# Adjacency stored for every second block of edges, index and weight per slot for the others

## What is computed

```python
# network 0, three layers (SAGE)
msg = relu(x[src] + edge_attr_16 @ emb)
s   = segment_sum(msg, dst, N)
x   = relu(s / count @ Wl + bl + x @ Wr)
# network 1, two layers (GIN)
agg = segment_sum(edge_weight[:, None] * x[src], dst, N)
x   = relu(agg @ W1.T) @ W2.T
# network 2: x[dst] * edge_attr_64 summed by dst; network 3: three attention layers
```

## Time and profile before

| | us |
|---|---|
| three runs | 12265.70, 12251.78, 12268.37 |
| median | 12265.7 |
| the profiled execution | 12279.62 |
| its span, first to last instruction | 12277.8 |
| first pass, in the trace | about 128 to 2830 |
| sage1, sage2 | 2900 to 3567, 3605 to 4258 |
| gin0, gin1 | 4327 to 4934, 4984 to 5600 |
| attention layers | 5760 to the end |

### The profile page before, as it was taken

How to read it: one execution, slowest core, us unless ns; L and a number is a source line. 1 busy time by engine, 2 the same in 40 slices (tenths; PEclk the granted TensorE clock), 3 DMA queues, 4 the chain that set the end, 5 groups by cost and what they waited for, 6 DMA issues and landing times. The chain is left out here.

```text
span 12277.8 us, 247904 instructions
## 1 busy us (share of the span) xinstructions
PE 9079.1 (74%) x82847; PEld 7960.6 (65%) x82848; DVE 7900.3 (64%) x23163; ACT 4425.0 (36%) x9728; POOL 7910.9 (64%) x8013
## 2 busy tenths in 40 slices
PE   4888888888989888886666666666666666666665
PEld 4777777776878788884555555455555555555554
DVE  6777777777989811105666666666666666666667
ACT  2545554454444300002333333333333333333332
POOL 5666666663767564551777777477777747777773
PEclk9888888888999999896555555555555555555555
DMA  4666666665989777672333333233333323333332
GB/s 140 185 185 183 185 185 186 183 176 151 260 223 254 208 262 258 222 261 67 95 95 96 96 96 96 64 94 96 96 96 96 96 64 94 96 96 96 96 96 53
DMA packets 1267061, 1740.59 MB, mean 142 GB/s; under 512 B 234569, under 2 KB 1001892, under 8 KB 1265547
## 3 DMA queue, kind: packets, MB, share of 16 engines
q1 hardware_dynamic: 610634, 718.01, 18.9%
q10 hardware_dynamic: 400704, 723.04, 18.7%
q0 software_dynamic: 254464, 283.59, 12.5%
HBM read 1366.51 MB, written 357.22 MB: 140 GB/s over the span
## 5 line engine op out<-in xcount | busy, mean ns | idle before, releaser
L2043 POOL DMA_INDIRECT rows<-gat_table,wgt x2457 | 2339.1, 952 | 962.3 <-issue 747.9
L2043 POOL DMA_INDIRECT Y<-gat_table,wgt x2394 | 2281.1, 953 | 729.6 <-issue 729.6
L937 POOL DMA_INDIRECT bins<-scratch,slots x1288 | 1316.6, 1022 | 960.5 <-issue 672.4
L2056 PE MATMUL scores<-ident,rep 128*128 128x128 f32 x2436 | 611.0, 428 | 1093.4 <-ACT rep L2139 1093.4
L2056 PE MATMUL scores<-ident,scratch 128*128 128x128 f32 x2415 | 605.7, 428 | 1030.3 <-ACT scratch L2139 1030.3
L2097 PE MATMUL bank<-sel,msg 128*72 128x32 f32 x9702 | 1308.6, 309 | 0.0
L1280 ACT ACTIVATE xT<-xT 112x256 f32<-112x256 f32 x1716 | 711.5, 415 | 1529.6 <-DVE xT L1122 1092.7
L2097 PEld LDWEIGHTS bank<-sel,msg 128*72 128x72 f32 x9702 | 1215.6, 237 | 44.5
L2056 PEld LDWEIGHTS scores<-ident,rep 128*128 128x128 f32 x2436 | 471.8, 223 | 1149.7 <-ACT rep L2139 1149.7
L1117 DVE TENSOR_TENSOR xT<-counts,xT 112x480 f32<-112x480 f32 x1716 | 1113.7, 649 | 118.6 <-issue 92.9
L1004 PE MATMUL bank<-xT 112*64 112x120 f32 (+1 forms) x13728 | 1166.1, 280 | 27.5 <-ACT xT L1280 26.3
(11 more groups left out here) (265 smaller groups left out, 19105.6 us busy)
## 6 DMA issues: line engine op xcount, KB each, us to landing
work<-in_dst_rows SPq DMA_DIRECT2D x693, 448.0 KB
xT<-bins ACTq DMA_DIRECT2D x1716, 119.0 KB
adj<-work ACTq DMA_DIRECT2D x598, 240.0 KB
work<-adj ACTq DMA_DIRECT2D x184, 780.0 KB
xT<-adj ACTq DMA_DIRECT2D x184, 780.0 KB
work<-near_table SPq DMA_DIRECT2D x1118, 128.0 KB
near_table<-work SPq DMA_DIRECT2D x598, 128.0 KB
bins<-zeros ACTq DMA_DIRECT2D x46, 1547.0 KB
```

The source lines that it names most:

```text
L937: nc.gpsimd.indirect_dma_start(bins, bass.IndirectOffsetOnAxis(slots[u % 2][:, r * G + j:r * G + j + 1], 0), binf[r][:, j, :], None).then_ ...
L2043: nc.gpsimd.indirect_dma_start(rows[s][:, j, :], None, gat_table, bass.IndirectOffsetOnAxis(edge_sources[:, g * G + j:g * G + j + 1], 0)). ...
L2056: last = nc.tensor.transpose(score_banks[s % 2][:, j * P:(j + 1) * P], reps[s % 2][:, j, :], ident[:])
```

## The change

Blocks with even number keep their adjacency as before; the table `adj` has 23 entries. For the odd blocks no `turned_cells`, `weigh`, `adjacency` or `keep` is run. In their place ACT copies the destination and the weight of each slot (`note`, 112 x 8 numbers a piece) and stores them once a block in `notes`.

`gin_pass` then takes one even and one odd block together, 23 pairs. The even block is summed from its adjacency as before, now into two halves in turn, with five load buffers in place of eight. The odd block is summed as sage1 does: `near_table` is loaded on the SP queue, `fetch` (three bf16 parts), `far_cells` and a new `weigh` (a multiplication by the weight) on DVE, `add_cells` into two halves, with rings of three buffers. DVE adds four half sums for each pair. The bf16 parts have to be made: `sage_dense(2)` and `gin_dense0` now split `x` too. The other loops are unchanged.

```diff
-        adj = dram("adj", (NBK, P, TS * MW))
+        adj = dram("adj", (PAIRS, P, TS * MW))
+        notes = dram("notes", (PAIRS, SL, TS * NOTE))
...
+            def solid(b):
+                return first_pass and b % 2 == 0
...
                             if first_pass and not (begun and i < 2):
-                                adjacency(*two_before(b, u, it, i))
+                                earlier_piece = two_before(b, u, it, i)
+                                if solid(earlier_piece[0]):
+                                    adjacency(*earlier_piece)
...
                             join(qn, k, s)
+                            if solid(b):
+                                turned_cells(qn, k, s)
                             if first_pass:
-                                turned_cells(qn, k, s)
...
                             rectify(qn, s)
-                            if first_pass:
+                            if solid(b):
                                 weigh(qn, k, s)
-                                if i > 1:
-                                    keep(b, u, it, i - 2)
-                                elif not (isinstance(b, int) and b == 0):
-                                    keep(*after(b, u, it, -1), NPC + i - 2)
+                            elif first_pass:
+                                note(qn, b, i, s)
+                            if i > 1 and solid(b):
+                                keep(b, u, it, i - 2)
+                            elif i < 2 and b and solid(b - 1):
+                                keep(*after(b, u, it, -1), NPC + i - 2)
...
+                    def note(qn, b, i, s):
+                        m = b // 2
+                        if i == 0:
+                            wait(ac, (s_notes[m % 2], 16 * (m // 2)))
+                        nc.scalar.activation(noted[m % 2][0:SL, i * PC * NOTE:(i + 1) * PC * NOTE].rearrange("p (k w) -> p k w", w=NOTE),
+                                             payf[s][0:SL, :, D + 1:D + 1 + NOTE], ACT.Copy).then_inc(q["noted"].handle, 1)
...
+            at_blocks, at_groups, add_at = [1, 4, 7, 10], [3, 9], 4
...
+                    def fetch(qn):
+                        i, s = qn % NPC, qn % RR
+                        wait(pe, (s_near[s], 16 * (qn // RR) + 16), (q["cells_ready"], qn - len(joint) + 1))
+                        for c in range(PC):
+                            for n, part_of in enumerate(parts_weighted):
+                                last = nc.tensor.matmul(joint[qn % len(joint)][0:SLW, c * D:(c + 1) * D], near_weighted[s][:, c * SLW:(c + 1) * SLW],
+                                                        part_of[:, i * PC + c, :], start=n == 0, stop=n == 2)
...
+                    for m in range(PAIRS):
+                        for i in range(NPC):
+                            qn = NPC * m + i
+                            fetch(qn)
+                            if i in at_blocks:
+                                add_piece(m, at_blocks.index(i))
+                            for n in groups_at(m, i):
+                                if n:
+                                    plain_sums(n - 1)
+                            if qn > 1:
+                                add_cells(qn - 2)
...
+                    def far_cells(qn):
...
+                        wait(ve, (q["cells_summed"], qn - R + 1))
...
+                    def weigh(qn):
...
+                        nc.vector.tensor_tensor(cellf[qn % R][0:SL, :, :], joint[qn % len(joint)][0:SL, 0:PC * D].rearrange("p (c d) -> p c d", d=D),
+                                                bc(notef[m % 2][0:SL, i * PC:(i + 1) * PC, 1], [SL, PC, D], 2), ALU.mult).then_inc(q["cells_ready"].handle, 1)
...
             last_one = i == 2
+            split = (X, parts_weighted, rests_apart) if last_one else (Y, Y_parts, rests)
...
-                            if c:
-                                rest(c - 1)
-                    if not last_one:
-                        rest(NCH - 1)
+                        if c:
+                            rest(ve, c - 1, *split)
+                    rest(ve, NCH - 1, *split)
```

More of the change, by code:

```diff
@@ new lines, in gin_pass, with groups_at @@
+            block_sums, cell_sums = [bank[5], bank[6]], [bank[0], bank[1]]
+            joint = [bank[3], bank[4], bank[2]]
+            plain_sum = bank[7][0:D, 0:WIN]
+            cellf = [c.rearrange("p (k w) -> p k w", w=D) for c in cells_weighted]
+            notef = [x.rearrange("p (k w) -> p k w", w=NOTE) for x in notes_in]
+            def groups_at(m, i):
+                return [n for j, n in enumerate(range(begin[m], begin[m + 1])) if at_groups[j] == i]
+            added = []
+            for m in range(PAIRS):
+                for i in range(NPC):
+                    added += [("group", n - 1) for n in groups_at(m, i) if n]
+                    if i == add_at and m:
+                        added += [("block", m - 1), ("cells", m - 1)]
@@ new lines, in add_cells @@
+                    def add_cells(qn):
+                        m, i = divmod(qn, NPC)
+                        wait(pe, (q["cells_ready"], qn + 1), (q["far_hot_ready"], qn + 1),
+                             *([(q["accumulated"], before["cells", m - 2] + 1)] if i == 0 and m > 1 else []))
+                        for c in range(PC):
+                            last = nc.tensor.matmul(half(cell_sums[m % 2], c % 2), cellf[qn % R][0:SL, c, :],
+                                                    far_weighted[qn % R][0:SL, c * MW:(c + 1) * MW],
+                                                    start=i == 0 and c < 2, stop=i == NPC - 1 and c >= PC - 2)
+                        last.then_inc(q["cells_summed"].handle, 1)
@@ new lines, in add_piece @@
+                    def add_piece(m, i):
+                        k = NGC * m + i
+                        s = k % NBL
+                        wait(pe, (s_block[s], 16 * (k // NBL) + 16),
+                             *([(q["accumulated"], before["block", m - 2] + 1)] if i == 0 and m > 1 else []))
+                        for c in range(GC):
+                            t = i * GC + c
+                            last = nc.tensor.matmul(half(block_sums[m % 2], t % 2), nodes[:, t, :], blocks[s][:, c * MW:(c + 1) * MW],
+                                                    start=t < 2, stop=t >= TS - 2)
+                        last.then_inc(q["blocks_summed"].handle, 1)
@@ L1419, in plain_sums @@
                                                     start=c == 0, stop=c == G - 1)
                         last.then_inc(q["sum_ready"].handle, 1)
-                    def body(b, u, it):
-                        for i in range(NGC):
-                            s, lap = laps(NGC, u, it, i, NBL)
-                            wait(pe, (s_block[s], 16 * lap + 16), *([(q["accumulated"], 2 * (b - 1))] if i == 0 else []))
-                            for c in range(GC):
-                                last = nc.tensor.matmul(sums[u % 2][0:D, 0:MW], nodes[:, i * GC + c, :], blocks[s][:, c * MW:(c + 1) * MW],
-                                                        start=i == 0 and c == 0, stop=i == NGC - 1 and c == GC - 1)
-                            last.then_inc(q["cells_summed"].handle, 1)
-                        if not (isinstance(b, int) and b == 0):
-                            plain_sums(b - 1, u - 1)
@@ L1436, in _ @@
+                    add_cells(pieces - 2)
+                    add_cells(pieces - 1)
+                    plain_sums(beside - 1)
+                    plain_sums(beside)
                 @block.vector
@@ L1472, in gin_pass @@
+                    plain_add(beside)
+                    accumulate(beside - 1)
+                    add_pair(PAIRS - 1)
+                    accumulate(beside)
             for s in range(RR):
                 s_rows[s].done(16 * G * slot_total(s, RR, n1))
+                s_near[s].done(16 * slot_total(s, RR, pieces))
+            for s in range(2):
+                s_notes[s].done(16 * slot_total(s, 2, PAIRS))
             for s in range(NBL):
-                s_block[s].done(16 * slot_total(s, NBL, NGC * B))
@@ L1711, in _ @@
                         nc.vector.tensor_copy(Y[:, c * TC:(c + 1) * TC, :], by_tile(turns_out[c % 2])).then_inc(q["tile_ready"].handle, 1)
+                        if c:
+                            rest(ve, c - 1, *split)
+                    rest(ve, NCH - 1, *split)
+                @block.gpsimd
+                def _(po):
+                    low(po, *split[1:])
                 @block.tensor
@@ L1727, in _ @@
                     hidden_act(ac, accT)
+                    for c in range(NCH):
+                        high_and_middle(ac, c, *split)
+                    middle(ac, NCH - 1, *split[1:])
                 @block.sync
```

248 lines of the change are left out of this document (160 added, 88 removed).

## The result

The changed kernel took 11796.3 us (median; 11785.5 to 11799.1) beside 12264.2 us for the kernel before (12251.8 to 12268.4) in the same session: a ratio of 0.9618, 95% interval 0.9602 to 0.9635. The forecast was 11730 us in a range of 11620 to 11880. So direction and range held, and the time came out 66 us above the forecast.

A forecast was written before the change was run, and what follows sets the result against it. The prediction took the chain between engines to bound the first pass and PE the gin passes, with DMA second. Its terms, -300 - 243 + 8 = -535 us, against the 12265.7 us median gave 11730 us, range 11620 to 11880.

The forecast's parts named there:

- the forecast's seven intervals: First pass, odd blocks: seven intervals between joins run at DVE's pace, each losing 0.60 us of turned cells, 4.2 us together.
- First pass, -300: First pass: odd blocks drop 13.3 us each to 45.4 us; 23 of them give 306, taken as 300 us.
- The flushes still bring the clock up and keep it up: First pass, odd blocks: PE has about 13 us less work, yet the flushes hold its clock up.
- PEclk 1.00 through the later two thirds of an odd block: First pass: sign to look for in the trace, PE's granted clock full in the later two thirds of odd blocks.
- the 102 that the forecast gave Pool at most: First pass: POOL needs at most 102 us for two blocks, which take 104 after the change; fits narrowly.
- (a): First pass: odd blocks give only DVE's share, PE staying longer at half clock; saving 180, 11851 us; 0.17 together with POOL rival.
- (e): First pass does not change since POOL sets it; in size like the DVE-share rival, 0.17 together with it.
- Gin passes, -243: Both gin passes: a pair of blocks takes 20.8 us, a pass 490 us instead of 607 and 616; gain 243 us.
- the row alone: Gin passes: a pair takes 19.4 us, counting the loss from fetch to sums but none for going back.
- (b): Gin passes held by gathers or loads at 24 us a pair: saving 103 in place of 243, 11870 us; chance 0.12.
- (d): Gin passes: PE's clock falls to 1.2 GHz, a pair takes 37 us, kernel slower than before at 12476 us; chance 0.02.
- Dense stages, +8: sage_dense(2) and gin_dense0: splitting x adds 5.9 us and a 1 us tail in the first, 1 us in the second.

The follow-up runs named there:

- e13: Changed kernel; first pass makes unused turned one-hots in odd blocks, gin0 issues 4 of 7 gathers, gin1 sums two of three parts: 11818.9 us, ratio 0.9656.
- e1: Changed kernel with SyncE issuing the first pass's wide attribute loads three pieces earlier: 11720.4 us, ratio 0.9555.
- e2: Kernel before the change with the wide attribute loads issued three pieces earlier: 12266.4 us, ratio 0.9998.
- e12: Changed kernel with attribute loads three pieces earlier, weighted passes two pieces at a time, source indices loaded in piece 9 of the block before: 11621.5 us, ratio 0.9493.
- e3: Changed kernel with TensorE taking its work two pieces at a time in both weighted passes: 11770.9 us, ratio 0.9596.

## Why the prediction held, and where it was off

- **What bounds the kernel.** The chain between engines in the first pass and PE in the gin passes: both held. In e13 VectorE's part of an odd block is 3.6 us, and 3.9 in the forecast's seven intervals themselves, for which it took 4.2.
- **First pass, -300.** The term that failed: it measured -247. The removal itself was, if anything, underrated: with the loads in time it is -318 (e1 against e2), an odd block 43.8 us. Piece 3 gave 3.5 us where 2.6 was taken, since its flush, which the forecast left "at half clock", went from 4.3 to 3.7 us. Piece 12 gave 1.9 where 2.3 was taken, and pieces 4, 10 and 11 gave 2.1 together in place of 2.8; e1 shows the late loads in these too. Piece 7 gave -0.6 in place of +1.4: 2.0 us there in 23 blocks are 47 us. The even blocks, 0.5 us longer each (why is not shown), account for 11 more, and the 6 us that the forecast had taken off its 306 come back, which leaves the 53. The step that failed is in the forecast's list of what could stand in the way: it weighed the stores, ScalarE's copies, Pool and the clock, but never SyncE, whose loads are issued a fixed number of pieces ahead. Pieces 5 and 6 shrank from 4.7 to 3.3 us, while a bin load takes 2.1 us (median) to land in the kernel before and 2.9 after. The trace of before held the sign: 48 short waits for `in_attr`, 24 us, not one over 1.2 us, of loads that arrive just in time.
- **The clock.** "The flushes still bring the clock up and keep it up" failed at piece 7 in 12 of 19 odd blocks; in the windows of block 29 it was 0.69 and 0.64. "PEclk 1.00 through the later two thirds of an odd block" was wrong for the changed kernel, where pieces 4 to 11 average 0.91, and right in e1, where they average 1.00.
- **Pool.** It fit: e1 and e12 took still more time out of the odd blocks (43.8 and 42.2 us) without Pool's coming in the way; in e12 an odd and an even block take 101.0 us together, less than the 102 that the forecast gave Pool at most. Rivals (a) and (e) are out; the term never came down to VectorE's share of 180.
- **Gin passes, -243.** Measured -236; 490.7 and 492.9 us against 490, pairs 20.56 us apart against 20.8. The parts were PE's: 13 x (0.46 + 0.56) + 4 x 1.44 + 2 x 0.8 = 20.6 us. The forecast by the row alone had been 19.4 and was lifted to 20.8 for Pool's sake; what made the difference was PE itself. Pool needs 14 x (1.064 + 0.30) = 19.1 us a pair. Eight sums take 0.56 us after a fetch and sixteen 0.97 (e3), so about 0.15 of each goes for the way back; the row's 1.79 us for 32 held one such return, and the forecast's 0.056 a sum had spread it over 32. It is the change of columns that costs, not that of the number type: in the earlier trace rows 24 fetches ahead of an f32 product over all 128 columns (L1017) take 0.71 us, 0.355 for twelve, and twelve ahead of sums over 64 take 0.45. The Trainium skill (TensorEngine Tiling (Array Packing), Key Properties) says that a change of tiling mode drains TensorE, which the forecast, with both directions counted, priced at 20.7 us a pair: the trace of the changed kernel agrees, and e3's 28 us less of PE time for half the changes agree too (13 changes x 23 pairs x 0.1 = 30). The rest of the match is luck: the pairs were 0.24 us shorter than taken, 5.5 us a pass, and start and end took 18 us in place of 12. The forecast's number was right by a reason that was partly wrong.
- **Rivals (b) and (d).** Neither showed: PE's clock in gin was 0.98, and e13 took away almost half the gathers for 3 us.
- **Dense stages, +8.** +6.4 and +0.2. A chunk of `sage_dense(2)` takes 4.17 us (3.60 in the earlier trace rows, 4.05 forecast). Thirteen times the difference is 7.4, more than the stage grew, so no tail shows:

```profile
4032.17 0.42 DVE L1767 TENSOR_TENSOR scratch<-bank,X 128x256 f32<-128x256 f32 x1
...
4036.34 0.42 DVE L1767 TENSOR_TENSOR scratch<-bank,X 128x256 f32<-128x256 f32 x1
```

- **The sum.** -535 forecast, -482 between the profiled spans and -468 between the medians. Of the 66 us between forecast and median, about 53 are the first pass, 7 the gin passes, -1 the dense stages and -6 the other stages, and 14 come from setting a sum worked out on one execution against a median that lay 14 us lower.

## What to carry to other kernels

When a change shortens the steps of a pipeline, list every transfer whose lead is counted in steps, turn the lead into microseconds after the change, and hold it against the transfer's time to landing; a load that is waited for often and briefly now is the first candidate to be late then. Look at the engine that issues it, even if the change doesn't touch it and it is never busy. And price a wait by what comes after it as well: here 1.5 us of waiting ahead of a flush came with 1.4 us more of TensorE's work behind it, at a fallen clock. When an edit takes busy time off the engine that sets a stage and the stage hardly gets shorter, look in that engine's own row of waits for what is new, before naming the next busiest engine.

## What the runs showed of the hardware

- A change between matmuls of 128 and of 64 columns costs TensorE about 0.1 us in each direction (0.46 against 0.355 us for twelve fetches, 0.56 against 0.41 for eight more sums in a run). A change from bf16 to f32 at 128 columns shows no such cost (0.355). Half as many changes took 28 us of 478 off its busy time.
- The same gather took Pool 0.960 us in the gin passes of before, 1.064 in those of after and 1.14 in e3. What makes it grow is not shown: from the gin passes of after to those of e3 the busy shares of TensorE and VectorE fell.
- The same flush of 32 matmuls took 3.44 us at a granted clock of 1.00 and 5.32 at about 0.64, after a wait of 2.9 us in which TensorE had been busy 0.23 of 2.50 us. After waits of about 1 us it took either: 3.44 in seven odd blocks of the changed kernel, 4.3 to 5.6 in six.
